# Scores of a local-attention layer with the first 64 queries of a head in one product, ahead of the mix, and a new order of stages on five engines

## The chip, the cores and the metric

The kernel runs on one core of one Trainium2 chip. The metric is the device time of one execution in microseconds (us). Everything is computed in fp32; a fp32 product appears in the trace as two pairs of a weight load (LDWEIGHTS, engine PEld) and a matrix multiplication (MATMUL, engine PE).

## The reference, cut to what matters

Input `x` is 32 batches of 128 tokens with 128 features. The reference runs a cross attention, then six local layers, then a second cross attention and a quantized linear layer. The change touches only the six local layers, which are about 80% of the time. Each layer is an attention with 16 heads of 64 features in windows of 32 tokens, and a gated feed-forward (MLP) after a LayerNorm:

```
def local_attention(q, k, v):
    w, nw = WINDOW, n // WINDOW            # 32 tokens, 4 windows
    ...
    bk2, bv2 = (look(bk), look(bv))        # the window and the one before it
    mask = (it < jb) | (it > jb + w) | (jb == -1)
    sim = jnp.einsum('bhwie,bhwje->bhwij', bq, bk2) * QK_SCALE
    sim = jnp.where(mask, -jnp.finfo(sim.dtype).max, sim)
    attn = jax.nn.softmax(sim, -1)
    out = jnp.einsum('bhwij,bhwje->bhwie', attn, bv2)
...
for i in range(DEPTH):                     # 6
    x = attn_layer(shift_tokens(x), Wqkv[i], q_scale[i], k_scale[i], Wo[i]) + x
    x = ffn_layer(shift_tokens(x), ln_g[i], ln_b[i], W1[i], b1[i], W2[i], b2[i]) + x
```

A query of window w sees the 64 keys of windows w-1 and w. In the kernel, the queries of windows 0 and 1 are both given keys 0 to 63, and the mask (`mask_band`) closes those that a query must not see.

## The kernel before

The function `local_layers` handles 192 units: 6 layers times 32 batches. A software pipeline runs over 206 steps; in each step every engine goes through a fixed list of stages, and a stage with lag L works in step s on unit s - L. Attention stages run once a unit, `project_out` once in two units, the MLP stages once in four (decorators `closing` and `second`). Engines wait for each other by semaphores only, so an engine executes its list strictly in order, and a stage that waits holds up all that stands behind it.

The stages on TensorE, with what they cost in instructions a unit:

- `project` (L733): q, k and v of a unit, 4 multiplications of 512 columns each.
- `transpose_qk` (L743): 8 transposes (16 multiplications of 128 columns), half of them for q and half for k.
- `scores` (L760): 64 products: for each of 8 pairs of heads `t`, each of the 4 windows, and both heads of the pair `j`. The 32 queries of a window are the weights, 64 keys move. The product stands on a tile of the array with 64 rows (the head) and 32 columns (the window). So eight tiles are in use, and each gets 8 products, 16 multiplications.
- `mix` (L787): 48 products on four tiles of 64 rows and 64 columns: values (64 x 64) as weights, 64 or 32 columns of turned probabilities move. Each tile gets 12 products, 24 multiplications.
- `project_out` (L801), 16 multiplications of 256 columns for two units; `mlp_mean` (L810), `mlp_variance` (L818), `mlp_up` (L828) and `mlp_down` (L839) for four units.

The results of TensorE lie in four pairs of PSUM banks. `ROTATING` (L610) gives the pairs out in turn, in the order of the stages on TensorE; a stage may fill its pair when the one that had it before has been read (`Banks.fill`).

Around TensorE, for one unit: ScalarE squares q and k (`square`), makes the reciprocal norms (`reciprocal_norms`), copies the transposes (`copy_qk`), v (`copy_v`) and the mix (`copy_mix`), and takes the exponentials. VectorE multiplies by the rotary tables (`products`, L1026 and L1027), sums the squares, adds the mask (`mask_scores`), takes row maxima and row sums, and turns the probabilities in blocks (`turn_probs`). GpSimd adds the rotary halves (`rotate`, L1154), multiplies by the norms (`normalise`, L1162), lowers the scores (`lower`) and normalises the probabilities (`normalise_probs`). The SP queue moves v (`place_v`) and the turned probabilities (`store_probs`, `place_probs`) by DMA.

Of the kernel before, what the change touches and what calls it, by code (L numbers as in the profile page):

```python
# [17 lines left out]
NB, S, D = 32, 128, 128  # L18
GB = 4
# [9 lines left out]
IT = INNER // P  # L29
# [89 lines left out]
def build(nc, dram):  # L119
    stack = ExitStack()  # L120
    with stack:
# [431 lines left out]
        def local_layers(phase):  # L553
            here = ExitStack()
            with here:
# [40 lines left out]
                for n in ("squared", "producted", "summed", "rotations", "normalised", "turned", "copied"))  # L596
# [13 lines left out]
            ROTATING = (("q", 0, 1), ("up2", 13, GB), ("mix", 6, 1), ("k", 0, 1), ("v", 4, 1), ("scores", 2, 1), ("out", 6, 2),  # L610
                        ("up0", 11, GB), ("mean", 7, GB), ("up1", 11, GB), ("variance", 10, GB), ("down", 13, GB), ("kT", 1, 1),
                        ("qT", 1, 1))
# [86 lines left out]
            def sp(sp):  # L699
                for step in range(UNITS + LAST):  # L700
# [4 lines left out]
                    if 0 < layer < DEPTH and into == 3:  # L705
                        load_v(sp, layer)
                    place_v(step - 4, sp)
# [9 lines left out]
            def pe(pe):  # L717
# [30 lines left out]
                def scores(u):  # L748
# [4 lines left out]
                    for t in range(IT):  # L753
                        for window in range(S // WIN):
                            these = slice(window * WIN, (window + 1) * WIN)
                            near = slice(max(window - 1, 0) * WIN, max(window + 1, 2) * WIN)
                            for j in range(2):
                                rows = slice(HD * j, HD * j + HD)
                                at = j * BANK + t * NEAR
                                mm = pe.matmul(  # L760
                                    pairs[i][these, at:at + NEAR], qkT[u % 2][rows, 0, t, these],
                                    qkT[u % 2][rows, 1, t, near], start=True, stop=True,
                                    tile_position=(rows.start, these.start))
# [79 lines left out]
                for step in range(UNITS + LAST):  # L843
                    project(step, 0)
                    mlp_up(step - 13, 2)
                    mix(step - 6)
                    project(step, 1)
                    project(step - 4, 2)
                    scores(step - 2)
                    project_out(step - 6)  # L850
                    mlp_up(step - 11, 0)
                    mlp_mean(step - 7)
                    mlp_up(step - 11, 1)
                    mlp_variance(step - 10)
                    mlp_down(step - 13)
                    transpose_qk(step - 1, 1)
                    transpose_qk(step - 1, 0)
                phase_end(pe)

            def act(act):  # L860
# [123 lines left out]
                for step in range(-1, UNITS + LAST):  # L984
                    square(step, 0)
                    reciprocal_norms(step - 1)
                    mlp_gelu(step - 13, 2)
                    mlp_affine(step - 11)
                    mlp_shift(step - 7)
                    square(step, 1)  # L990
                    copy_mix(step - 6)
                    copy_v(step - 4)
                    exponentials(step - 4)
                    prepare(step + 1)
                    mlp_log(step - 10)
                    mlp_root(step - 10)
                    mlp_gelu(step - 11, 0)
                    mlp_gelu(step - 11, 1)
                    mlp_square(step - 9)
                    copy_qk(step - 1, 1)  # L1000
                    copy_qk(step - 1, 0)
                phase_end(act)

            def dve(dve):
# [107 lines left out]
                for step in range(UNITS + LAST):  # L1112
                    if step < UNITS and step % NB == 0:
                        start_layer(step // NB)
                    products(step, 0)
                    turn_probs(step - 5)
                    mlp_hidden(step - 13, 2)
                    products(step, 1)
                    mask_scores(step - 2)
# [780 lines left out]
```

## Time and profile before

| | |
|---|---|
| median of 3 runs | 3405.78 us (3400.22 to 3406.63) |
| profiled execution: time | 3404.29 us |
| profiled execution: span | 3402.5 us |
| mean granted TensorE clock | 0.982 |
| PE busy | 3247.4 us (95%) |
| DVE busy | 2942.0 us (86%) |
| POOL busy | 2640.0 us (78%) |
| ACT busy | 2379.8 us (70%) |
| PEld busy | 2059.5 us (61%) |

The span runs from the first to the last instruction; the 1.8 us between it and the time lie outside. A busy PE is not a PE at its peak: the recorded duration of a multiplication includes its way through the array, and successive ones overlap. So a stage is sized here from its start to the start of the next stage, never by the sum of its durations.

### The profile page before, as it was taken

To read this page: it belongs to the slowest core of one execution; us is meant where nothing else is said; L and a number is where in the kernel's file an instruction comes from. 1 tells how busy PE (TensorE), PEld (TensorE's weight loads), DVE (VectorE), ACT (ScalarE), POOL (GpSimd) and SP (SyncE) were. 2 spreads that over 40 slices of the span, in tenths; PEclk is the share of its full clock that TensorE was granted. 3 is DMA by queue.
4 is the path that set the end of the run, shared out by engine and by line. 5 is a ranking of instruction groups with operands and counts; after the bars stand their busy time and mean duration, and the time that the engine had idled before them with its cause. 6 is when DMAs were issued, how large, how long until landed. Compare 5 with 4: busy or idle time off the path is not lost. (4 is left out here: it accounts for less than half of the span.)

```text
span 3402.5 us, 130907 instructions
## 1 busy us (share of the span) xinstructions
PE 3247.4 (95%) x56355; PEld 2059.5 (61%) x56386; DVE 2942.0 (86%) x3343; ACT 2379.8 (70%) x4288; POOL 2640.0 (78%) x1408
## 2 busy tenths in 40 slices
PE   8977999999999999999999999999999999977996
PEld 4544666666666666666666666666666666643554
DVE  6869999999999999999989899998999999935887
ACT  6865676767676667777677776776767676746895
POOL 1218988888888888888888888888888888833576
PEclk9989999999999999999999999999999999988998
DMA  2001433333433343333433334343344333340000
GB/s 94 2 1 56 121 114 114 121 121 115 119 112 114 120 126 120 114 114 122 126 111 117 114 111 129 117 120 114 114 126 126 118 111 113 109 125 1 2 11 17
DMA packets 229189, 336.06 MB, mean 99 GB/s; under 512 B 39046, under 2 KB 151044, under 8 KB 228228
## 3 DMA queue, kind: packets, MB, share of 16 engines
q1 hardware_dynamic: 228612, 327.68, 31.5%
q8 instruction: 446, 7.31, 0.9%
q14 instruction: 131, 1.07, 0.1%
HBM read 124.14 MB, written 102.76 MB: 67 GB/s over the span
## 5 line engine op out<-in xcount | busy, mean ns | idle before, releaser
L733 PE MATMUL psum<-w_qkv,f_xs 128*128 128x512 f32 x2304 | 1078.3, 604 | 12.3 <-DVE f_times_sin L1027 7.6
L1154 POOL TENSOR_TENSOR f_rotated<-f_times_cos,f_times_sin 128x1024 f32<-128x1024 f32 x384 | 908.4, 2366 | 8.8 <-DVE f_times_sin L1027 8.8
L1162 POOL TENSOR_TENSOR f_rotated<-f_rotated,f_rnorm 128x1024 f32<-128x1024 f32 x384 | 723.0, 1903 | 31.8 <-ACT f_rnorm L908 4.9
L733 PEld LDWEIGHTS psum<-w_qkv,f_xs 128*128 128x128 f32 x2304 | 409.8, 191 | 395.1 <-issue 375.2
L897 ACT ACTIVATE f_squares<-psum 128x1024 f32<-128x1024 f32 x384 | 393.0, 1023 | 341.0 <-PE psum L733 335.9
L1146 POOL TENSOR_TENSOR f_probs<-f_probs,f_rowsum 128x1024 f32<-128x1024 f32 x192 | 365.4, 1903 | 322.3 <-DVE f_rowsum L1066 322.3
L1026 DVE TENSOR_TENSOR f_times_cos<-psum,rot 128x1024 f32<-128x1024 f32 x384 | 470.0, 1224 | 121.8 <-ACT f_squares L897 117.7
L915 ACT COPY f_qkT<-psum 128x1024 f32<-128x1024 f32 x384 | 369.9, 1013 | 210.2 <-PE psum L743 210.2
L1027 DVE TENSOR_TENSOR f_times_sin<-psum,rot 128x1024 f32<-128x1024 f32 x384 | 466.4, 1214 | 0.0
L1034 DVE TENSOR_REDUCE f_sumsq<-f_squares 128x16 f32<-128x1024 f32 x384 | 463.8, 1210 | 0.0
L743 PEld LDWEIGHTS psum<-consts,f_rotated 128*128 128x128 f32 x3072 | 348.6, 141 | 96.3 <-issue 87.6
L743 PE MATMUL psum<-consts,f_rotated 128*128 128x128 f32 x3072 | 371.2, 274 | 16.2 <-POOL f_rotated L1162 13.3
L1140 POOL TENSOR_TENSOR f_probs<-f_probs,f_negmax 128x1024 f32<-128x1024 f32 x192 | 365.0, 1901 | 0.0
L787 PEld LDWEIGHTS psum<-f_probsT,f_v 64*64 64x64 f32 x6144 | 262.7, 135 | 162.5 <-issue 162.5
L801 PE MATMUL psum<-f_outT,w_o 128*128 128x256 f32 x1536 | 358.9, 387 | 1.2 <-ACT f_outT L929 1.2
L760 PEld LDWEIGHTS psum<-f_qkT 64*32 64x32 f32 x24576 | 254.0, 105 | 146.9 <-issue 143.1
L787 PE MATMUL psum<-f_probsT,f_v 64*64 64x64 f32 (+1 forms) x6144 | 309.7, 228 | 15.6 <-issue 15.6
L801 PEld LDWEIGHTS psum<-f_outT,w_o 128*128 128x128 f32 x1536 | 285.8, 191 | 45.2 <-issue 1.8
L787 PE MATMUL psum<-f_probsT,f_v_moved 64*64 64x32 f32 (+1 forms) x12288 | 307.1, 217 | 0.0
L760 PE MATMUL psum<-f_qkT 64*32 64x64 f32 x24576 | 285.2, 226 | 1.3 <-issue 1.3
L787 PEld LDWEIGHTS psum<-f_probsT,f_v_moved 64*64 64x64 f32 x12288 | 285.8, 136 | 0.0
L828 PE MATMUL psum<-f_xn,w 128*128 128x512 f32 (+1 forms) x576 | 278.3, 607 | 7.4 <-ACT f_xn L971 7.4
(175 smaller groups left out, 5173.5 us busy)
## 6 DMA issues: line engine op xcount, KB each, us to landing
f_v_moved<-f_v SPq DMA_DIRECT2D x768, 128.0 KB, 2.8
turned_blocks<-w_qkv SPq DMA_DIRECT2D x192, 512.0 KB, 3.0
f_probsT<-turned_blocks SPq DMA_DIRECT2D x768, 128.0 KB, 2.8
w_qkv<-in_l_wqkv SPq DMA_DIRECT2D x18, 512.0 KB, 4.2
w_o<-in_l_wo SPq DMA_DIRECT2D x6, 512.0 KB, 4.5
w_qkv<-in_ctxT SPq DMA_DIRECT2D x1, 2048.0 KB, 8.7
out<-x_f_result SPq DMA_DIRECT2D x8, 256.0 KB, 2.2
w<-in_l_w SPq DMA_DIRECT2D x6, 341.0 KB
```

The lines of the kernel that those rows point to most:

```text
L733: mm = pe.matmul(pairs[i][:, j * BANK:(j + 1) * BANK], xs[g % 2][:, u % GB, :], w_qkv[:, part * INNER + j * BANK:part * INNER + (j + 1) * ...
L743: tr = pe.transpose(pairs[i][:, t * S:(t + 1) * S], rotated[u % 2][:, part, 2 * t:2 * t + 2, :].rearrange("p h d -> p (h d)"), ident)
L760: mm = pe.matmul(pairs[i][these, at:at + NEAR], qkT[u % 2][rows, 0, t, these], qkT[u % 2][rows, 1, t, near], start=True, stop=True, tile_p ...
L787: mm = pe.matmul(pairs[i][cols, at + windows.start * WIN:at + windows.stop * WIN], values, probsT[u % 2][rows, windows, j, :], start=True, ...
L801: mm = pe.matmul(pairs[i][:, 0:GT // 2], w_o[:, t, :], outT[:, t, tokens], start=t == 0, stop=t == IT - 1)
L897: act.activation(squares[part][:, :], pair("qk"[part], u), ACT.Square).then_inc(squared[part], 1)
L915: act.copy(qkT[u % 2][:, part].rearrange("p t n -> p (t n)"), pair(("qT", "kT")[part], u)).then_inc(copied[part], 1)
L1026: dve.tensor_tensor(halves(times_cos[part][:, :]), halves(taken), table(0), ALU.mult)
L1027: dve.tensor_tensor(halves(times_sin[part][:, :]), halves(taken)[:, ::-1], table(1), ALU.mult).then_inc(producted[part], 1)
L1034: dve.tensor_reduce(sumsq[u % 2][:, part * H:(part + 1) * H], squares[part][:, :].rearrange("p (s h d) -> p h s d", s=2, h=H), axis=XY, op ...
L1154: pool.tensor_tensor(rotated[u % 2][:, part].rearrange("p h (s d) -> p s h d", s=2), halves(times_cos[part][:, :]), halves(times_sin[part] ...
L1162: pool.tensor_tensor(rt, rt, rnorm[u % 2][:, part * H:(part + 1) * H].unsqueeze(2).broadcast_to([P, H, HD]), ALU.mult).then_inc(normalised ...
```

## The change

1. `scores` makes 48 products instead of 64. First, for every pair of heads, the products of windows 2 and 3 as before, on tiles of 64 rows and 32 columns (array columns 64 to 127; four tiles). Then, for every pair of heads, one product with the first 64 queries of a head as weights against keys 0 to 63, on a tile of 64 rows and 64 columns (array columns 0 to 63; two tiles). The numbers written to PSUM are the same.
2. On TensorE `scores` stands directly ahead of `mix`. Before, `mix`, then `project` for k and v, then `scores` stood in this order.
3. All engines have a new order of stages, and some lags change: v 4 to 3 (with its copy and its placing), exponentials and row sums 4 to 3, `lower` 3 to 2, both rotations in the unit's own step, up2 and its gelu 13 to 12, the statistics of the MLP earlier or later by one or two. `mix`, `turn_probs`, `project_out` and `mlp_down` keep theirs.

```diff
@@ banks
-            ROTATING = (("q", 0, 1), ("up2", 13, GB), ("mix", 6, 1), ("k", 0, 1), ("v", 4, 1), ("scores", 2, 1), ("out", 6, 2),
-                        ("up0", 11, GB), ("mean", 7, GB), ("up1", 11, GB), ("variance", 10, GB), ("down", 13, GB), ("kT", 1, 1),
-                        ("qT", 1, 1))
+            ROTATING = (("mean", 9, GB), ("q", 0, 1), ("up2", 12, GB), ("scores", 2, 1), ("mix", 6, 1), ("k", 0, 1), ("up0", 11, GB),
+                        ("v", 3, 1), ("up1", 11, GB), ("out", 6, 2), ("down", 13, GB), ("qT", 1, 1), ("kT", 1, 1), ("variance", 9, GB))
@@ sp
-                    if 0 < layer < DEPTH and into == 3:
+                    if 0 < layer < DEPTH and into == 2:
                         load_v(sp, layer)
-                    place_v(step - 4, sp)
+                    place_v(step - 3, sp)
@@ scores
-                    for t in range(IT):
-                        for window in range(S // WIN):
-                            these = slice(window * WIN, (window + 1) * WIN)
-                            near = slice(max(window - 1, 0) * WIN, max(window + 1, 2) * WIN)
-                            for j in range(2):
-                                rows = slice(HD * j, HD * j + HD)
-                                at = j * BANK + t * NEAR
-                                mm = pe.matmul(
-                                    pairs[i][these, at:at + NEAR], qkT[u % 2][rows, 0, t, these],
-                                    qkT[u % 2][rows, 1, t, near], start=True, stop=True,
-                                    tile_position=(rows.start, these.start))
+                    one, two, both = (slice(2 * WIN, 3 * WIN), slice(WIN, 3 * WIN)), (slice(3 * WIN, 4 * WIN), slice(2 * WIN, 4 * WIN)), \
+                        (slice(0, 2 * WIN), slice(0, 2 * WIN))
+                    for windows in ((one, two), (both,)):
+                        for t in range(IT):
+                            for these, near in windows:
+                                for j in range(2):
+                                    rows = slice(HD * j, HD * j + HD)
+                                    at = j * BANK + t * NEAR
+                                    mm = pe.matmul(pairs[i][these, at:at + NEAR], qkT[u % 2][rows, 0, t, these],
+                                                   qkT[u % 2][rows, 1, t, near], start=True, stop=True,
+                                                   tile_position=(rows.start, these.start))
@@ pe
                 for step in range(UNITS + LAST):
+                    mlp_mean(step - 9)
                     project(step, 0)
-                    mlp_up(step - 13, 2)
+                    mlp_up(step - 12, 2)
+                    scores(step - 2)
                     mix(step - 6)
                     project(step, 1)
-                    project(step - 4, 2)
-                    scores(step - 2)
+                    mlp_up(step - 11, 0)
+                    project(step - 3, 2)
+                    mlp_up(step - 11, 1)
                     project_out(step - 6)
-                    mlp_up(step - 11, 0)
-                    mlp_mean(step - 7)
-                    mlp_up(step - 11, 1)
-                    mlp_variance(step - 10)
                     mlp_down(step - 13)
+                    transpose_qk(step - 1, 0)
                     transpose_qk(step - 1, 1)
-                    transpose_qk(step - 1, 0)
+                    mlp_variance(step - 9)
@@ act
                     square(step, 0)
+                    mlp_gelu(step - 12, 2)
                     reciprocal_norms(step - 1)
-                    mlp_gelu(step - 13, 2)
-                    mlp_affine(step - 11)
+                    copy_mix(step - 6)
+                    square(step, 1)
+                    exponentials(step - 3)
+                    mlp_gelu(step - 11, 0)
+                    mlp_affine(step - 10)
+                    prepare(step + 1)
+                    mlp_square(step - 9)
+                    copy_v(step - 3)
+                    mlp_gelu(step - 11, 1)
+                    copy_qk(step - 1, 0)
+                    copy_qk(step - 1, 1)
                     mlp_shift(step - 7)
-                    square(step, 1)
-                    copy_mix(step - 6)
-                    copy_v(step - 4)
-                    exponentials(step - 4)
-                    prepare(step + 1)
-                    mlp_log(step - 10)
-                    mlp_root(step - 10)
-                    mlp_gelu(step - 11, 0)
-                    mlp_gelu(step - 11, 1)
-                    mlp_square(step - 9)
-                    copy_qk(step - 1, 1)
-                    copy_qk(step - 1, 0)
+                    mlp_log(step - 9)
+                    mlp_root(step - 9)
@@ dve
+                    turn_probs(step - 5)
                     products(step, 0)
-                    turn_probs(step - 5)
-                    mlp_hidden(step - 13, 2)
+                    mlp_hidden(step - 12, 2)
+                    sum_squares(step, 0)
+                    mask_scores(step - 2)
                     products(step, 1)
-                    mask_scores(step - 2)
-                    sum_squares(step, 0)
-                    mlp_centre(step - 7)
-                    add_out(step - 6)
+                    sum_squares(step, 1)
                     mlp_hidden(step - 11, 0)
                     add_down(step - 13)
-                    sum_squares(step, 1)
+                    row_sums(step - 3)
+                    add_out(step - 6)
                     mlp_hidden(step - 11, 1)
-                    row_sums(step - 4)
+                    row_maxima(step - 2)
+                    mlp_centre(step - 8)
                     clamp_norms(step)
-                    row_maxima(step - 2)
@@ pool
-                    rotate(step - 1, 1)
+                    normalise(step - 1, 0)
                     normalise(step - 1, 1)
-                    normalise(step - 1, 0)
-                    lower(step - 3)
                     rotate(step, 0)
-                    mlp_scale(step - 10)
                     normalise_probs(step - 4)
+                    rotate(step, 1)
+                    lower(step - 2)
+                    mlp_scale(step - 9)
```

## Rows read from the trace of the kernel before

**Rows 1.** The page's second part: busy tenths in 40 slices.

```profile
PE   8977999999999999999999999999999999977996
DVE  6869999999999999999989899998999999935887
POOL 1218988888888888888888888888888888833576
PEclk9989999999999999999999999999999999988998
```

**Rows 2.** Windows of the local layers: us, busy (instructions), clock, DMA.

```profile
core 0: us, PE busy (x) PEld busy (x) DVE busy (x) ACT busy (x) POOL busy (x), PEclk, DMA share, GB/s
316.00:2990.00 2674.00, 2657.89 (x49582) 1702.40 (x49583) 2426.29 (x2577) 1879.45 (x2359) 2329.35 (x1167) 1.00 0.39 118
1500.00:1557.00 57.00, 57.00 (x1063) 36.55 (x1062) 51.51 (x56) 40.34 (x52) 49.92 (x25) 1.00 0.37 113
```

**Rows 3.** The waits of PE: waited for, us in total, times, longest.

```profile
PE psum L743 <- POOL f_rotated L1162: 13.3, 10, 6.2
PE psum L733 <- DVE f_times_sin L1027: 7.6, 5, 1.5
```

**Rows 4.** The timeline of PE, four steps of the middle: start, us, work.

```profile
1501.00 0.27 PE L787 MATMUL psum<-f_probsT,f_v 64*64 64x64 f32 x1
...
1502.53 3.70 PE L733 MATMUL psum<-w_qkv,f_xs 128*128 128x512 f32 x8
1506.16 1.48 PE L760 MATMUL psum<-f_qkT 64*32 64x64 f32 x128
1507.58 3.72 PE L801 MATMUL psum<-f_outT,w_o 128*128 128x256 f32 x16
...
1513.74 1.88 PE L733 MATMUL psum<-w_qkv,f_xs 128*128 128x512 f32 x4
1515.55 0.27 PE L787 MATMUL psum<-f_probsT,f_v 64*64 64x64 f32 x1
...
1526.53 1.91 PE L743 MATMUL psum<-consts,f_rotated 128*128 128x128 f32 x16
1528.27 1.88 PE L733 MATMUL psum<-w_qkv,f_xs 128*128 128x512 f32 x4
...
1559.85 3.70 PE L733 MATMUL psum<-w_qkv,f_xs 128*128 128x512 f32 x8
```

**Rows 5.** The timeline of the weight loads (PEld), from k's projection to project_out.

```profile
1503.07 0.19 PEld L733 LDWEIGHTS psum<-w_qkv,f_xs 128*128 128x128 f32 x1 [0.24 <-issue]
...
1505.21 0.19 PEld L733 LDWEIGHTS psum<-w_qkv,f_xs 128*128 128x128 f32 x1 [0.24 <-issue]
1506.16 1.32 PEld L760 LDWEIGHTS psum<-f_qkT 64*32 64x32 f32 x128 [0.76 <-issue]
1507.58 0.94 PEld L801 LDWEIGHTS psum<-f_outT,w_o 128*128 128x128 f32 x5
```

**Rows 6.** The timeline of PE in one mix: the same place in successive t.

```profile
1501.13 0.35 PE L787 MATMUL psum<-f_probsT,f_v_moved 64*64 64x64 f32 x10
...
1501.48 0.35 PE L787 MATMUL psum<-f_probsT,f_v_moved 64*64 64x64 f32 x10
...
1501.83 0.35 PE L787 MATMUL psum<-f_probsT,f_v_moved 64*64 64x64 f32 x10
```

**Rows 7.** The timeline of PE in the second cross attention, four tiles of 32 columns.

```profile
3206.75 1.08 PE L1361 MATMUL psum<-x_probsT,x_vpad 128*32 128x128 f32 x32
3207.65 1.06 PE L1365 MATMUL psum<-x_probsT,x_ones 128*32 128x128 f32 x32
3208.64 0.66 PE L1347 MATMUL psum<-consts,x_expo 128*128 128x128 f32 x4
```

**Rows 8.** The timeline of ACT, the copies of the transposes in one step.

```profile
1527.60 1.93 ACT L915 COPY f_qkT<-psum 128x1024 f32<-128x1024 f32 x2 [0.18 <-PE psum L743]
```

**Rows 9.** The timeline of PE at the end of the local layers.

```profile
3040.92 5.45 PE L801 MATMUL psum<-f_outT,w_o 128*128 128x256 f32 x16 [1.20 <-ACT f_outT L929]
3046.21 1.02 PE L818 MATMUL psum<-f_spread,mean_mat 128*128 128x512 f32 x2
3050.94 3.40 PE L828 MATMUL psum<-f_xn,w 128*128 128x512 f32 x4 [3.72 <-ACT f_xn L971]
3054.14 1.32 PE L810 MATMUL psum<-f_mlp_xs,mean_mat 128*128 128x512 f32 x2
...
3063.19 1.02 PE L818 MATMUL psum<-f_spread,mean_mat 128*128 128x512 f32 x2
```

**Rows 10.** The timeline of PE at the start of the local layers.

```profile
275.10 1.48 PE L760 MATMUL psum<-f_qkT 64*32 64x64 f32 x128
277.01 1.06 PE L743 MATMUL psum<-consts,f_rotated 128*128 128x128 f32 x8 [0.43 <-POOL f_rotated L1162]
278.88 1.06 PE L743 MATMUL psum<-consts,f_rotated 128*128 128x128 f32 x8 [0.80 <-POOL f_rotated L1162]
```

## Prediction

> **What bounds the kernel now.** I read the page first. Its slices show PE at nine tenths or more from a tenth of the span to its last eighth, with the clock full there, and DVE at nine in most of the same slices [rows 1]. Two engines could be the bound, so the next view is the windows. Over 316 to 2990 us PE is busy in 2658 of 2674 us, and in 57 us of the middle in all of them; DVE is busy in 51.5 of those 57 and POOL in 49.9 [rows 2]. A busy PE may still hide short waits, so the third view is PE's own waits: outside the filling of the pipeline there is almost nothing. The five waits for `products` (7.6 us together) are as many as there are later layers, where VectorE first remakes the rotary tables [rows 3]. The reader should take from this that in the local layers PE's instructions follow each other without a gap. What PE's list costs is the step, and a step is worth (1559.85 - 1502.53)/4 = 14.3 us [rows 4]. VectorE would be the bound only below 14.3 x 51.5/57 = 12.9 us.
>
> **The blocks of tiles before.** The fourth view is PE's timeline, read from start to start. The unit of 32- and 64-column tiles costs: `mix` 1502.53 - 1501.00 = 1.53, `scores` 1507.58 - 1506.16 = 1.42 [rows 4]. Going in and out also costs. Multiplications of 512 columns follow each other at (1505.21 - 1503.07)/5 = 0.428 [rows 5]. Four of them would be 1.71, but q ahead of the mix takes 1515.55 - 1513.74 = 1.81 [rows 4]: 0.10 for going in. Eight would be 3.42, but k and v between mix and scores take 3.63 [rows 4]: 0.21, of which 0.10 is again the way in and 0.11 the first full weight load after the mix, which could not be made ahead. The weight loads show the same thing: those of L733 come ahead of their multiplications, that of L760 after 0.76 us of idleness [rows 5]. Before, a unit has two such blocks: 2 x 0.10 + 2 x 0.11 + 1.42 + 1.53 = 3.37 us.
>
> **What sets the pace inside a block.** In the mix six multiplications a tile take 0.35 us (1501.13, 1501.48, 1501.83), so a round over the four tiles takes 0.058 whether 64 or 32 columns move [rows 6]. It is set by the weight load of 64 columns. 24 rounds are 1.40; the other 0.13 of 1.53 is the emptying of the array. On four tiles of 32 columns with 128 columns moving, 32 multiplications take 3207.65 - 3206.75 = 0.90, eight rounds of 0.112 [rows 7]. Multiplications on one tile follow each other at the pace of their moving columns; tiles beside it are free. Half the columns, as in the scores, would be 0.056 a round. So a stage costs its rounds, the multiplications on its fullest tile, and not its count. Old scores: 16 rounds on eight tiles, floor 0.90, plus 0.13, against 1.42 seen; the remaining 0.39 I take for the supply of 128 pairs.
>
> **Step 1, the new scores.** The products of windows 2 and 3 keep 16 rounds, now on four tiles: 16 x 0.056 = 0.90. The products of 64 queries are 16 rounds on two tiles; a round is the larger of 0.056 (64 moving) and 0.058 (64 weight columns): 0.93. A quarter of the multiplications goes, and the rounds double, because two tiles idle while four work and the other way round. Count alone would give 96/128 x 1.42 = 1.07, a gain of 0.35; a round as slow as in the old scores (1.42/16 = 0.089) would give 2.84. Both are bounds. I take the rounds, since on four tiles 32 multiplications cost 0.028 each and not 0.011 [rows 7].
>
> **Step 2, between the two halves.** No row shows a change from 32 to 64 columns with the other side of the array free. The nearest show that the array empties when the tiling changes: 0.13 behind the last round. The bounds are 0 and 0.13; I take 0.13, since every change of tiling in the trace has it. The Trainium skill, TensorEngine Tiling (Array Packing), section Tiling Modes, says that a change of mode, not just of tile, drains TensorE. The trace agrees for the changes from and to the full array, 0.10 to go in and 0.13 to go out; whether it holds between two tilings no run here shows.
>
> **Step 3, mix directly behind.** The second half and the mix have the same tiling, so the mix follows at the pace of rounds; one way in (0.10) and one exposed weight load (0.11) go. Sum after: 0.10 + 0.90 + 0.13 + 0.93 + 1.53 + 0.11 = 3.70. Against 3.37: **+0.33 us a unit**.
>
> **Step 4, the new order.** While PE has no wait, order is worth nothing by itself. I went through the semaphores of the new lists with the starts of the timeline. The tightest wait is `scores` for `copy_qk`: in a step with neither up2 nor mean, only q's projection (1.71 to 1.81) lies between the last transpose and the scores. The two copies end 1527.60 + 1.93 = 1529.53, and the transposes end at 1528.27 [rows 4, 8]: 1.26 us behind them, so about half a microsecond is left. ScalarE is at 40 of 57 us [rows 2], and in the new list all gelus of a group stand between two uses of the other table, so it loads tables half as often. Behind the scores would wait mix, k and all that follow, but the cover holds. Others: the pair of q is needed again by v, three stages later, when `products` has had over 5 us; DMAs keep a step and more. VectorE's table making at a layer's start now stands ahead of `turn_probs` and `products`; its 1.5 us a layer [rows 3] stays within +-1 us a layer, +-5 in all. I take 0.
>
> **Step 5, both ends.** At the start PE waits for the rotations [rows 10], so the first units hide what scores cost more: 187 of 192 pay. 187 x 0.33 = 62. At the end, before, the last variance but one stands behind the last project_out, and `mlp_up` waits 3.72 us for it; 4.7 us (3046.21 to 3050.94) lie on the chain, and from the last mean to its variance 3063.19 - 3054.14 = 9.0 us with up and down between [rows 9]. In the new order that variance runs a step ahead of project_out and the last one follows its mean with only down between. Bounds 0 and 12 us gained; I take 8.
>
> **Sum**, against the profiled execution (span 3402.5 and 1.8 outside, 3404.3): 3404.3 + 62 - 8 = **3458 us**. It stood 1.5 us under the median of the runs, so nothing is added. That is 1.5% slower.
>
> **The rivals.**
>
> *The halves run beside each other (faster).* If no emptying lies between, and a tile takes its products as they come, the 64-query products fill array columns 0 to 63 while the others are still at work. They can't start before half of the supply that the old scores needed: 128 weight loads begin within 1.32 - 0.11 = 1.21 us [rows 5], so 64 in 0.61. Then a unit is 0.10 + 0.61 + 0.93 + 1.53 + 0.11 = 3.28, 0.09 less than before: 3404 - 17 - 8 = 3379. Faster supply could bring more, down to VectorE's 12.9 us. It decides at a start 0.70 us after the first product (0.74 with the gain at the end); after that the change loses. For it: the eight tiles of the old scores do run beside each other. Against: every change of tiling seen empties the array. Chance 0.17.
>
> *No emptying, but in order.* The halves follow each other directly: 0.13 less, +0.20 a unit, 37 us: 3404 + 37 - 8 = 3433. The Trainium skill, TensorE: Matmul & The Clock Gate, Part 3, says that multiplications start and end in program order, which would forbid the first rival; no row here separates it. Chance 0.08.
>
> *A new wait in the new order.* Should the copies land 1 us later than step 4 has them, three steps of four wait some 0.5 us ahead of the scores: 144 x 0.5 = 72 us more, 3530. Against it speak ScalarE's idleness and the half microsecond left. Chance 0.05.
>
> **How the numbers follow.** The forecast (rounds, with emptying) has 0.70 and by itself 3435 to 3490: the gain at the end 0 to 12, layer starts +-5, the round of the first half 0.053 to 0.060, some 10 us each way, and an emptying between tilings dearer by 0.05, 10 us. The range 3420 to 3500 adds the second rival and small waits and leaves out the first rival and the large wait, 2 in 10. What can be told from no change in this kernel is about 0.2%, 7 us. Faster holds the first rival and a little of the extremes, 0.18; same 0.03; slower 0.79.
>
> **What would show it.** In the profile after: L760's (the new line's) weight loads 96 a unit; from the first score product to the first of the mix 1.9 to 2.0 us, with a gap of 0.1 before the 64-query products; mix still 1.5; no wait in front of mix; a step of about 14.6 us and PE without gaps in it; DVE's share down. It is wrong if the 64-query products start within 0.7 us of the first (first rival), if the scores take near 1.1 us (count, not rounds), or if PE shows waits for f_qkT in each step.

## The result, and the profile after

The changed kernel takes 3558.61 us (median of 4 runs, 3541.9 to 3566.56) against 3406.2 for the kernel before; the ratio is 1.0444 (95% interval 1.0404 to 1.0484). It is slower, as forecast, but by 152 us where 52 were forecast, and outside the stated range.

The page of the kernel after, first line and the busy tenths that answer to [rows 1]:

```profile
span 3564.7 us, 118527 instructions
...
PE   8979999999999999999999999999999999987996
...
DVE  6869988888888888888888888888878888854787
```

DVE has fallen from nine tenths to eight, PE looks as full as before. The windows, with the same columns as [rows 2]: first the local layers, then the scores and the mix of one unit, then those of the next:

```profile
316.00:3150.00 2834.00, 2750.32 (x43360) 1827.75 (x43359) 2406.44 (x2566) 1769.38 (x2260) 2319.07 (x1162) 0.99 0.37 110
1513.74:1515.69 1.95, 1.95 (x97) 1.86 (x98) 1.19 (x2) 1.37 (x3) 1.95 (x2) 1.00 0.36 145
1515.69:1517.22 1.53, 1.53 (x104) 1.49 (x100) 1.53 (x3) 0.00 (x0) 1.53 (x2) 1.00 0.39 158
1527.77:1529.72 1.95, 1.95 (x97) 1.86 (x98) 0.85 (x2) 1.37 (x3) 1.18 (x2) 1.00 0.50 204
1529.72:1532.97 3.25, 1.83 (x105) 1.68 (x101) 3.25 (x4) 0.00 (x0) 3.25 (x2) 1.00 0.12 44
```

PE is now idle for 84 us of these 2834, where before it was idle for 16 of 2674. The scores take 1.95 us in both units and the first mix 1.53: these are the forecast's own terms. The second mix takes 3.25 us for the same instructions, and PE is busy in only 1.83 of them. PE's timeline shows where the rest is, in the second mix, behind two thirds of its products (start, us, work, idle before and its releaser):

```profile
1527.77 2.12 PE L760 MATMUL psum<-f_qkT 64*32 64x64 f32 x94
...
1529.68 0.27 PE L786 MATMUL psum<-f_probsT,f_v 64*64 64x64 f32 x1
...
1529.72 0.22 PE L760 MATMUL psum<-f_qkT 64*64 64x64 f32 x2
...
1530.54 0.36 PE L786 MATMUL psum<-f_probsT,f_v_moved 64*64 64x32 f32 x11
...
1532.39 0.24 PE L786 MATMUL psum<-f_probsT,f_v_moved 64*64 64x32 f32 x1 [1.42 <-issue]
1532.39 0.27 PE L786 MATMUL psum<-f_probsT,f_v 64*64 64x32 f32 x2
...
1532.97 0.70 PE L732 MATMUL psum<-w_qkv,f_xs 128*128 128x512 f32 x1
```

The stage's semaphore waits all stand ahead of its first product. So an idle stretch of 1.42 us behind two thirds of its products can't be a wait for data or for banks, and the trace puts it down to "issue": the engine waited for nothing that the profile shows. In PE's waits this line is by far the longest of the kernel after (first fence). The kernel before has two such lines (second fence). The wait of 1.3 us stands between two products of one `scores`. The nine of 15.6 us all stand ahead of a mix's first product, five of them before 410 us and four behind 2990 us, where the pipeline fills and empties; they are waits of a stage whose releaser the profile doesn't name. Of the 84 in the kernel after, 81 are inside a mix; the longest, 3.7 us, is one of the three that are not:

```profile
PE psum L786 <- issue: 81.9, 84, 3.7
```

```profile
PE psum L787 <- issue: 15.6, 9, 4.6
PE psum L760 <- issue: 1.3, 1, 1.3
```

The DMA view of the kernel after, for 1529.90 to 1530.95 us (first fence, up to 1.44 us ahead of the product that ends the idle stretch) and for 1530.95 to 1532.39 us (second). A queue of kind "instruction" brings the engines' own program; q8 is TensorE's, as the count below shows:

```profile
DMA packets 23, 0.05 MB, mean 43 GB/s; under 512 B 15, under 2 KB 15, under 8 KB 22
...
q1 hardware_dynamic: 22, 0.03, 9.1%
q8 instruction: 1, 0.02, 5.5%
```

```profile
DMA packets 6, 0.02 MB, mean 17 GB/s; under 512 B 0, under 2 KB 0, under 8 KB 6
...
q1 hardware_dynamic: 6, 0.02, 4.7%
```

One block of instructions lands just before this idle stretch, at 1530.93 us, and none during it. I counted a gap wherever two successive multiplications inside scores and mix start more than 0.35 us apart. The kernel after has 85 gaps, 97 us together. Each ends 1.21 to 1.66 us after the last block on queue q8 landed; in 24 of them, longer ones, the block lands inside the gap. The queue's blocks have one size, over the whole kernel:

```profile
q8 instruction: 398, 6.52, 0.8%
```

6.52 MB in 398 packets are 16.4 KB each. The trace holds 101,976 instructions of TensorE (weight loads, multiplications and semaphore instructions), 256 a block.

The trace also tells where in the program the gaps lie. Number TensorE's instructions in the order of their starts, and let k be the number of blocks landed by the end of a gap. Then the first instruction behind the gap is number 256 k + 162, in all 85 gaps. So TensorE stops exactly where one block ends and goes on when the next is there.

My reading (theory I): TensorE's program arrives in blocks, and scores and mix together are a run of 384 short instructions in 3.5 us, weight loads and multiplications together, which is used up sooner than blocks arrive. The rival (theory D): the mix got its data or banks late, or the new order did it in some other way.

### The profile page after: what moved, and what is told of

Its sections match the earlier page's. It is cut to its first block, busy times and chain, and to the rows that moved or that the text cites. A ratio compares the mean times of both kernels' runs of the same rounds, so it can differ in the third digit from the quotient of the medians.

```text
span 3564.7 us, 118527 instructions
## 1 busy us (share of the span) xinstructions
PE 3355.9 (94%) x50211; PEld 2197.8 (62%) x50242; DVE 2932.1 (82%) x3343; ACT 2274.4 (64%) x4196; POOL 2639.1 (74%) x1408
## 3 DMA queue, kind: packets, MB, share of 16 engines
q8 instruction: 398, 6.52, 0.8%
## 4 chain that ended last, share of the span: by engine, by line
PE 85%; issue 6%; DVE 4%; ACT 3%; POOL 1%; SPq 0%; DMA 0%; POOLq 0%; DVEq 0%; ACTq 0%
PE psum L732 28%; PE psum L760 11%; PE psum L800 9%; PE psum L742 9%; PE psum L786 8%; PE psum L827 7%; PE psum L838 3%; ACT x_expo L1479 1%; PE psum L817 1%; PE psum L809 1%; PE psum L309 1%; PE psum L1336 1%; PE psum L1346 1%; ACT x_expo L391 1%; DVE x_negmax L472 1%
## 5 line engine op out<-in xcount | busy, mean ns | idle before, releaser
L732 PE MATMUL psum<-w_qkv,f_xs 128*128 128x512 f32 x2304 | 1096.9, 609 | 10.0 <-issue 4.6
L732 PEld LDWEIGHTS psum<-w_qkv,f_xs 128*128 128x128 f32 x2304 | 419.5, 192 | 444.2 <-issue 432.8
L928 ACT COPY f_outT<-psum 128x1024 f32<-128x1024 f32 x192 | 194.4, 1013 | 461.9 <-PE psum L786 461.9
L760 PEld LDWEIGHTS psum<-f_qkT 64*32 64x32 f32 x18432 | 374.6, 116 | 167.5 <-issue 149.2
L760 PE MATMUL psum<-f_qkT 64*32 64x64 f32 x18432 | 419.1, 219 | 2.0 <-issue 1.0
L786 PE MATMUL psum<-f_probsT,f_v_moved 64*64 64x32 f32 (+1 forms) x12288 | 334.8, 216 | 58.7 <-issue 58.5
L786 PE MATMUL psum<-f_probsT,f_v 64*64 64x32 f32 (+1 forms) x6144 | 333.7, 226 | 24.1 <-issue 23.4
L800 PEld LDWEIGHTS psum<-f_outT,w_o 128*128 128x128 f32 x1536 | 294.5, 192 | 84.2 <-issue 45.3
L786 PEld LDWEIGHTS psum<-f_probsT,f_v_moved 64*64 64x64 f32 x12288 | 304.2, 134 | 63.7 <-issue 63.0
L786 PEld LDWEIGHTS psum<-f_probsT,f_v 64*64 64x64 f32 x6144 | 296.3, 134 | 29.8 <-issue 28.3
```

Of the source, the lines that this page charges most:

```text
L732: mm = pe.matmul(pairs[i][:, j * BANK:(j + 1) * BANK], xs[g % 2][:, u % GB, :], w_qkv[:, part * INNER + j * BANK:part * INNER + (j + 1) * ...
L760: mm = pe.matmul(pairs[i][these, at:at + NEAR], qkT[u % 2][rows, 0, t, these], qkT[u % 2][rows, 1, t, near], start=True, stop=True, tile_p ...
L786: mm = pe.matmul(pairs[i][cols, at + windows.start * WIN:at + windows.stop * WIN], values, probsT[u % 2][rows, windows, j, :], start=True, ...
L800: mm = pe.matmul(pairs[i][:, 0:GT // 2], w_o[:, t, :], outT[:, t, tokens], start=t == 0, stop=t == IT - 1)
```

## The experiments

The ratios of the experiments are to runs of the kernel before on the same chip, and gaps are counted as above.

**1. Cut the run in two.** The changed kernel with one long stage between scores and mix (the bank rotation and two of ScalarE's stages swapped to suit):

```diff
                     scores(step - 2)
-                    mix(step - 6)
                     project(step, 1)
+                    mix(step - 6)
```

> The changed kernel with k's projection between scores and mix (TensorE, bank rotation; on ScalarE square of k ahead of copy_mix). Theory I, instruction supply: the 1 to 2 us gaps inside the mix (about 112 us in all in the changed kernel, 82 gaps over 0.35 us) come because scores and mix together are a run of 384 short instructions that is used up faster than the next 16 KB of instructions arrive. With 3.4 us of long multiplications cut into that run the gaps go, and one more pair of tiling changes is paid, 0.34 us x 187 = 63 us: 3558 - 112 + 63 = about 3510 us (3495 to 3525), next to no gap inside a stage. Rival D, data or banks of the mix are late: the gaps stay, 3558 + 63 = about 3620 us.

3501.69 us, ratio 1.0289 (1.0263 to 1.0314); 2 gaps left, 1.9 us. (What lies between is k's projection alone, 1.8 us; the expectation wrote 3.4.) Less than 2 us of long multiplications, and one more pair of tiling changes, make the kernel 57 us faster. The timeline of this kernel, one unit's scores, k, and the place of the mix ahead of the next line (from start to start, 2.11 us for scores and its emptying, and 3.45 for k and the mix together):

```profile
1503.15 2.18 PE L760 MATMUL psum<-f_qkT 64*32 64x64 f32 x96
1505.26 1.98 PE L732 MATMUL psum<-w_qkv,f_xs 128*128 128x512 f32 x4
1508.71 1.98 PE L827 MATMUL psum<-f_xn,w 128*128 128x512 f32 x4
```

Theory I had 3510, theory D 3620. The mix's data and banks are the same, but it also runs 1.8 us later, which by itself would help late data; that no gap of the changed kernel is such a wait is shown by where they lie, inside a stage and on the edge of a block, and by experiment 10. By the times the gaps are then worth 57 + 63 = 120 us, the 63 being the forecast price of the extra changes (116 with the two ratios in place of the two times).

**2. Only the order.** The changed kernel with the old `scores` loop (64 products), directly ahead of the mix.

> The changed kernel, all lists and lags, with the old 64 products of scores on eight tiles, directly ahead of the mix. By rounds alone a unit costs 0.21 us less than in the kernel before (one way in and one exposed weight load): 3404 - 39 - 8 = 3357 us. Theory I: the run of short instructions is now 448 in 3 us instead of 384 in 3.5, so there are more and longer gaps than in the changed kernel: 150 to 250 us of them, 3510 to 3600 us. Rival D: gaps as in the changed kernel at most, 112 us: 3470 us or less.

3746.44 us, ratio 1.1032 (1.0984 to 1.1079). It has 157 gaps, 284 us, the longest 3.96, more than theory I's own range. By rounds alone it should have been faster than the kernel before. Part of what is missing lies outside the gaps: the granted clock fell in the local layers, 0.96 in this window against 1.00 before [rows 2]:

```profile
330.00:3350.00 3020.00, 2762.22 (x49340) 1779.86 (x49339) 2407.54 (x2562) 1771.07 (x2261) 2313.64 (x1159) 0.96 0.34 104
```

The clock has two levels, 1.2 and 2.4 GHz. The profile's clock records put 232 us of this window at the lower one, which costs at most half of them, 116 us. Now the sum closes: 3357 by rounds, 284 in gaps and 116 of clock are 3757, measured 3746. The changed kernel has the same in small: 34 us of its local layers at the lower level, at most 17 us lost. Seven of those nine stretches begin in a gap of 1.7 us or more or within 1.6 us behind it. Behind one, the eight multiplications of k and v take 5.40 us where they took 3.70 before [rows 4]; k's four start 0.85 us apart, v's again 0.43:

```profile
537.48 5.40 PE L732 MATMUL psum<-w_qkv,f_xs 128*128 128x512 f32 x8
```

The local layers of the kernel before and of experiments 1, 3, 4 and 6 have no time at the lower level.

**3. Only the new scores.** The kernel before, its order and lags, with the new loop over `windows` in `scores`.

> The kernel before, its order and lags, with the new scores alone (48 products, 32 columns then 64). By rounds: 1.03 + 0.93 + 0.13 = 2.09 us instead of 1.42, +0.67 x 187 = 125 us: 3529 us (3515 to 3545), and, by theory I, hardly a gap inside a stage, since scores and mix are apart. If products cost by their count, 1.07 us and a time below 3406. If it was the new order that slowed the changed kernel, 3470 or less.

3523.97 us, ratio 1.0361 (1.0339 to 1.0383), no gap. A unit's scores, in this kernel's timeline:

```profile
1507.52 2.18 PE L761 MATMUL psum<-f_qkT 64*32 64x64 f32 x96
1509.62 1.98 PE L828 MATMUL psum<-f_xn,w 128*128 128x512 f32 x4
```

The scores take 2.10 us from start to start, forecast 2.09, before 1.42 [rows 4]. A quarter fewer products cost half as much again. That is the price of the rounds alone.

**4. Change the tiling more often.** The changed kernel with the two loops of `scores` swapped:

```diff
-                    for windows in ((one, two), (both,)):
-                        for t in range(IT):
+                    for t in range(IT):
+                        for windows in ((one, two), (both,)):
```

> The changed kernel with the loop over pairs of heads outermost in scores: for each pair four products on tiles of 32 columns, then two on tiles of 64 columns, the same products otherwise. If every change of tiling empties the array, a pair costs 2 x 0.056 + 0.13 + 2 x 0.058 + 0.13 = 0.49 us and up to 0.09 for weight loads that can't be made ahead, so scores 3.9 to 4.6 instead of 1.96 and the kernel about 3800 to 3950 us. If tiles of different width run side by side, the two kinds overlap, scores take about 1 us and the kernel gets faster than 3450 us.

3812.7 us, a single run. The timeline of this kernel, first and last row of one unit's scores and the stage behind the mix:

```profile
1502.96 4.07 PE L760 MATMUL psum<-f_qkT 64*32 64x64 f32 x94
1506.86 0.22 PE L760 MATMUL psum<-f_qkT 64*64 64x64 f32 x2
...
1508.39 1.98 PE L732 MATMUL psum<-w_qkv,f_xs 128*128 128x512 f32 x4
```

Scores and mix together take 1508.39 - 1502.96 = 5.43 us; less the 1.53 of a mix in the changed kernel, that is 3.90 us for the same 96 multiplications that took 1.95. Fourteen more changes of tiling cost 1.95 us, 0.14 each, though the two kinds stand on different sides of the array. So the array empties also between tiles of 32 and of 64 columns, and there is nothing of the first rival. The Trainium skill, TensorEngine Tiling (Array Packing), section Tiling Modes, says that changing the mode drains TensorE; here the runs agree, with 0.13 to 0.14 us a time. Only 6 gaps are left: with 384 short instructions spread over 5.5 us, the blocks keep up.

**5. The old scores with the run cut.** The kernel of experiment 1 with the old scores.

> The lists and lags of the changed kernel with the old 64 products, and k's projection between scores and mix. The tiling changes and instructions are those of the kernel before, so TensorE's list costs the same, and no gaps are expected; what is left is the shorter end of the local layers, 8 us: 3406 - 8 = about 3398 us (3385 to 3404). If the new lists cost something of their own that the other runs hid, 3410 or more.

3454.28 us, ratio 1.0148 (1.0122 to 1.0174). My expectation of 3398 missed. It holds 62 gaps, 65.5 us, 26 in scores and 36 in mix (the 37th wait of the second row stands ahead of a mix at the emptying of the pipeline), and 3398 + 65.5 is 3464:

```profile
PE psum L759 <- issue: 28.8, 26, 2.6
PE psum L786 <- issue: 25.5, 37, 2.2
```

The old scores are 256 short instructions in 1.42 us. With the mix 1.8 us behind them that is too dense; with k and v between, 3.6 us, as in the kernel before, it is not. So not every cut makes a run harmless. I take the length of the long work between for the reason; the two kernels also differ in the order of the other stages.

**6. Less traffic on the DMA queues.** The changed kernel, whose transfers of v and of the probabilities are cut to 16 columns after the first units, so that its output is wrong:

```diff
+                n = HALFV if u < 4 else 16
-                sp.dma_start(dst[0:HD, 0, :], src[HD:, 0, :]).then_inc(v_placed, 16)
+                sp.dma_start(dst[0:HD, 0, 0:n], src[HD:, 0, 0:n]).then_inc(v_placed, 16)
...
```

> The changed kernel, but from the fifth unit on the transfers of v, and from the third those of the probabilities, move 16 columns a partition instead of 512, 1024 or 256; the output is wrong for it, TensorE's instructions stay. If the gaps come from the run of short instructions alone, a block of instructions is still used up sooner than the next one arrives (transfers of 16 KB at 0.9 us at best and some 1.4 us until its first instruction starts), and most of the 112 us stays: 3500 to 3550 us. If it is the data transfers that hold up the instructions' transfers, the gaps go: about 3450 us.

3495.52 us, ratio 1.0273 (1.0238 to 1.0308); 79 gaps, 58.6 us, none longer than 1.35. The number of gaps stays, their length falls from 1.14 to 0.74 us in the mean. The missing block's own transfer hardly changed, 1.17 us in the mean in the gaps of the changed kernel and 1.07 here. But it began earlier: 0.74 us (median) behind the first instruction of the block before it, where that was 1.13. The time is 63 us shorter: 38 us of gaps and up to 17 us of clock, which here never falls; the last 8 us are open. Both theories in the expectation have a part: the run of short instructions makes the gaps, and the kernel's own transfers lengthen them.

**7. One tiling, half the rounds.** The kernel of experiment 1, with the last 64 queries of a head in one product too (window 2 against other keys, so its scores and the output are wrong):

```diff
-                    for windows in ((one, two), (both,)):
+                    low, high = (slice(0, 2 * WIN), slice(0, 2 * WIN)), (slice(2 * WIN, 4 * WIN), slice(2 * WIN, 4 * WIN))
+                    for windows in ((low, high),):
```

> The split kernel (k between scores and mix), with the last 64 queries of a head also in one product, against keys 64 to 127; the scores of window 2 are then with other keys, the output is wrong for it. Four tiles of 64 columns, 32 products, one tiling. By rounds: 16 x 0.058 = 0.93 instead of 0.90 + 0.13 + 0.93 = 1.96 us, so 1.03 x 187 = 193 us under the split kernel: 3502 - 193 = about 3310 us (3295 to 3325). By count of products the step from 48 to 32 would save at most 0.4 us a unit, 75 us: 3425.

3330.04 us, ratio 0.9786 (0.976 to 0.9812): 172 us less than experiment 1, 193 forecast by rounds, 75 at most by count. The scores of one unit in this kernel's timeline:

```profile
1502.73 1.16 PE L759 MATMUL psum<-f_qkT 64*64 64x64 f32 x64
1503.83 1.98 PE L732 MATMUL psum<-w_qkv,f_xs 128*128 128x512 f32 x4
```

They take 1.10 us where experiment 1 took 2.11. With all four tiles in use, products of 64 queries would pay; window 3 needs keys that window 2 doesn't, in the same columns, and I found no layout in which both keep their numbers.

**8. The shorter end for the kernel before.** Its scores and its order mix, k, v, scores, with variance at lag 9, up2 at 12, v at 2, and lists on the other engines rearranged.

> The kernel before: its scores, and mix, k, v, scores in this order, so that both runs of short instructions stay apart; but with lags as in the changed kernel where they shorten the end of the local layers (variance 9, up2 12) and v at lag 2, and the lists on the other engines arranged to suit. TensorE's list costs the same, so the middle stays. The tail after the last transpose was 87.2 us in the kernel before and 73 to 74 in the changed and split ones; if it shortens here as there, the time is 3406 - 10 to 18 = about 3392 us (3385 to 3400). If the short tail came with the other order only, 3406; if the new lists make TensorE wait in each step, over 3412.

3538.25 us, ratio 1.0401 (1.0383 to 1.042). My expectation missed, for another reason: its 2 gaps are 1.7 us, but TensorE now waits for semaphores in the middle, which [rows 3] did not have:

```profile
PE psum L786 <- issue: 45.5, 55, 2.5
PE psum L742 <- DVE f_times_sin L1026: 31.5, 44, 2.8
PE psum L800 <- ACT f_outT L928: 31.1, 7, 7.1
PE psum L759 <- DVE f_times_sin L1026: 25.6, 5, 5.2
```

Of the 55 waits in the first row 54 (44.5 us) stand ahead of a mix's first product, over the whole length and not on the edge of a block: the stage waits, and the profile doesn't say for what. A bank pair was wanted again before `products` had read it, and project_out came before ScalarE had copied the mix. The clock is at the lower level for 72 us here.

**9. The shorter end, lags only.** The kernel before with no list reordered:

```diff
-                    mlp_variance(step - 10)
+                    mlp_variance(step - 9)
...
-                    mlp_square(step - 9)
+                    mlp_square(step - 8)
-                    mlp_affine(step - 11)
+                    mlp_affine(step - 10)
```

(and 9 for 10 in `mlp_log`, `mlp_root`, `mlp_scale` and the banks.)

> The kernel before, all orders kept, but the statistics of the MLP one step earlier: lag 9 instead of 10 for variance, its logarithm and root and for mlp_scale, 8 instead of 9 for mlp_square, 10 instead of 11 for mlp_affine. In the middle nothing changes; at the end the last variance but one runs ahead of the last project_out instead of behind it. The 87.2 us from the last transpose to the last mlp_down should become about 76, the time 3400 - 11 = 3389 us (3383 to 3397). If the tail is set by something else, 3400; if the earlier statistics make an engine wait in each group, 3410 or more.

3410.48 us, ratio 1.0006 (0.9993 to 1.002): no difference. The end did shorten. In the kernel before, the last transposes start at 2989.42 and the last mlp_down at 3076.66 (87.2 us):

```profile
2989.42 0.82 PE L743 MATMUL psum<-consts,f_rotated 128*128 128x128 f32 x6
...
3076.66 2.81 PE L839 MATMUL psum<-f_gelu,w 128*128 128x512 f32 x6 [1.65 <-DVE f_gelu L1101]
```

and in this one at 3003.67 and 3081.36 (77.7 us), but project_out waits for the copy of the mix, 10.5 us where it was one wait of 1.2:

```profile
3003.67 1.58 PE L743 MATMUL psum<-consts,f_rotated 128*128 128x128 f32 x13
...
3081.36 2.81 PE L839 MATMUL psum<-f_gelu,w 128*128 128x512 f32 x6 [1.65 <-DVE f_gelu L1101]
```

```profile
PE psum L801 <- ACT f_outT L929: 10.5, 6, 2.7
```

The sixth of these waits, 1.2 us, is the one of the kernel before. The other five lie in the middle, one in each later layer, and give 9.3 of the 9.5 us back.

**10. Double the suspected run.** The kernel before, with every product of scores made twice into the same place, mix as far from them as before:

```diff
-                    for t in range(IT):
+                    for t in (*range(IT), *range(IT)):
```

> The kernel before with all 64 products of scores made twice, the same into the same places; mix far from them as before. By the tiles alone a unit costs 1.42 - 0.13 = 1.29 us more, 1.29 x 187 = 241 us: about 3641 us. By instruction supply a run of 512 short instructions in 2.8 us uses up two blocks of 256 one after the other, each at most 1.4 us long, while a block comes every 3 to 4 us: gaps of 2 us or more a unit inside scores, the time over 3950 us. If gaps need the mix (its data, its banks), none appear inside scores.

4192.63 us, a single run; 179 gaps, 409.7 us, all inside scores. Each ends on the edge of a block, at instruction 256 k + 193. Tiles alone give 3641; the clock's lower level holds for 287 us of the local layers (0.96 granted in the window below), at most 143 us lost, and 3641 + 410 + 143 = 4194. First the window, then, from the timeline, one unit's scores, whose 256 multiplications take 5.1 us instead of 2.7:

```profile
1000.00:3500.00 2500.00, 2224.84 (x53026) 1461.87 (x53024) 1771.37 (x1869) 1368.30 (x1715) 1680.16 (x843) 0.96 0.31 92
```

```profile
1999.46 2.06 PE L760 MATMUL psum<-f_qkT 64*32 64x64 f32 x186
2003.69 0.95 PE L760 MATMUL psum<-f_qkT 64*32 64x64 f32 x70 [2.18 <-issue]
2004.57 0.70 PE L801 MATMUL psum<-f_outT,w_o 128*128 128x256 f32 x2
```

The gaps need neither the mix nor the new order. They come where short instructions are dense. In the gaps of experiments 1, 2, 5 and 6, too, and in the one of the kernel before, TensorE goes on at number 256 k + 162. Side by side, with the short instructions of scores and mix in the second column, and what lies between them; the last column but one is half of the time at the lower clock level, the most that it can cost:

| kernel | short instructions (us) | gaps | us in gaps | us of clock | time, us |
|---|---|---|---|---|---|
| before | 192 (1.5), 3.6 us of k and v, 256 (1.4) | 1 | 1.5 | 0 | 3394 to 3414 |
| 3: new scores, old order | 192 (1.5), 3.6 us, 192 (2.1) | 0 | 0 | 0 | 3524 |
| 1: run cut | 192 (2.1), 1.8 us of k, 192 (1.5) | 2 | 1.9 | 0 | 3502 |
| 5: run cut, old scores | 256 (1.4), 1.8 us, 192 (1.5) | 62 | 65.5 | 1 | 3454 |
| changed kernel | 384 (3.5) | 85 | 97.0 | 17 | 3559 |
| 2: old scores next to mix | 448 (3.0) | 157 | 284.1 | 116 | 3746 |
| 10: scores twice | 512 (2.7) | 179 | 409.7 | 143 | 4193 |

## Why the prediction was right and wrong

**What bounds, and step 1 (rounds):** right. TensorE's list is the step. Scores forecast 0.90 + 0.13 + 0.93 = 1.96 us, measured 1.95; alone in the old order 2.09 and 2.10 (experiment 3). Count alone is refuted by experiments 3 and 7.

**Step 2 (emptying between the tilings):** right, 0.13 taken and 0.14 a time measured in experiment 4. With it the first and the second rival fall. What the prediction set against the first, that multiplications start in program order, is not what rules it out: in the profile after, the mix's first product starts at 1529.68 and the last two of the scores, which stand ahead of it in the program, at 1529.72. Between tiles of one tiling starts do change places; between two tilings the emptying forbids it.

**Step 3 (mix directly behind, +0.33 us a unit):** the sum of tiles was right. Experiment 1 has the same instructions as the changed kernel, hardly a gap, and pays one pair of changes more: 3502 measured, 3458 + 63 = 3521 by the prediction's terms. But the step is also where it failed. It counted what the join saves, one way in and one exposed weight load, and not what it makes: a run of 384 short instructions. The supply of instructions was priced at nothing. The prediction had itself put 0.39 us of the old scores down to "the supply of 128 pairs"; that is a steady cost of every unit and not a late block, but it named the thing to ask about. And among PE's waits before stood a single one between two scores products with no releaser, 1.3 us. Neither was followed up. The term that was missing is 120 us by experiment 1's account. The trace gives 97 in counted gaps, 5 in five late blocks in other stages and at most 17 of clock. It is the whole of the miss: 3458 + 120 = 3578, 19 above the measured time, as experiment 1 was 19 below its sum.

**Step 4 (the new order is worth nothing, no wait ahead of the scores):** right for semaphores. `scores` waits for `copy_qk` twice, 0.7 us in all, and the third rival, a new wait in the new order, did not come. Its 3530 lies nearer to the measured time than the forecast's 3458, but by another cause. "Mix still 1.5" was right for the mixes without a gap only. What I had not asked of the order is how it spreads instructions over time.

**Step 5 (both ends):** undersized. From the last transposes to the last mlp_down it is 73.4 us in the changed kernel (3165.14 to 3238.55), 87.2 before: 13.8 us gained, where 8 were taken and 12 was the bound. That is 6 of the 19 us by which the sums stand too high. The start gives another 6: the scores of the ninth unit begin at 375.80 us before, at 369.35 in experiment 1 and at 370.18 in the changed kernel. The rest lies in the middle: from there to the 185th unit, experiment 1 takes 0.63 us a unit more than the kernel before, where the sum has 0.67, 7 us in all.

**The size:** 152 us measured against 52. The direction and its chance (0.79 for slower) rested on the rounds and held.

How far ahead a block is asked for can be read from the trace. In the local layers of the changed kernel the transfer of a block never starts sooner than 40 instructions ahead of the first one of the block before it, and in the kernel before never sooner than 45. So at most one block is on its way or waiting. In both kernels such a transfer takes 0.88 us at the least, and the block's first instruction starts no sooner than 1.2 us after it has landed. What stays open is what holds the transfer's start back; its median in the changed kernel is 74 instructions behind that first one. The runs only bracket what is harmless: 256 short instructions in 1.4 us are with 3.6 us of long ones beside them and not with 1.8; 192 are with 1.8. No version here that keeps the output beats the kernel before: experiment 9 is equal to it within its interval.

## What to carry to other kernels

On a tiled TensorE, with two or four tiles at work, a stage here cost 0.056 to 0.058 us for each multiplication on its fullest tile (of 64 columns moving and at most 64 as weights) plus 0.13 us of emptying for each change of tiling. With eight tiles the old scores took 1.42 us and not the 1.03 of this rule. Fewer, larger products lose when they leave tiles idle. Before two stages of short instructions are put next to each other to save a change of tiling, count instructions over time: 384 in 3.5 us ran ahead of their own fetching here, and the stall shows as idleness "issue" in the middle of a stage, where the program has no wait. To tell it from a late semaphore, see whether all such stalls lie at one place modulo 256 in the engine's instructions. Long stalls of this kind cost more than their own length, since the clock falls behind some of them. When a single small effect in the trace has no explanation, price what happens when the change makes it common.

## What the runs showed of the hardware that was not expected

TensorE stalls on its own program. In every one of the 85 gaps of the changed kernel the first product came 1.21 to 1.66 us after a 16.4 KB block of instructions had landed, and in experiment 10 (179 gaps) it was 1.21 to 1.67. Every gap ends on the edge between two blocks, and no more than one block is fetched ahead. The Trainium skill, Runtime: NRT & Kernel Launch, section Instruction fetch mechanics, says that programs are refilled in 16 KiB blocks of 256 instructions, the next while the current one runs, and calls the cost mostly hidden. The block's size agrees (6.52 MB in 398 packets); "mostly hidden" holds for the kernel before (1.5 us) and not for these runs (up to 410 us, and up to 143 us of clock behind them). The kernel's own data transfers take part: with them cut down, the gaps of the changed kernel shrank from 97.0 to 58.6 us.
